# Two small attentions: VectorE's row maxima moved ahead of the step's side work

## The reference

```python
# layer 0, cross attention ("c0"): 32 heads of 16, rotated q and k, no mask
q = (x @ Wq).reshape(b, n, 32, 16); k, v = jnp.split(ctx @ Wkv, 2, axis=-1)
q, k = apply_axial_rope(q, pos_map), apply_axial_rope(k, ctx_pos_map)
w = softmax(einsum('bqhd,bkhd->bhqk', q, k) * scale)
x = layernorm(x + einsum('bhqk,bkhd->bqhd', w, v).reshape(b, n, 512) @ Wout + bout)
# layer 1, self attention ("a1"): 16 heads of 32, 4 key/value groups, causal
x = layernorm(x + causal_softmax_attention(x @ Wq, x @ Wk, x @ Wv) @ Wo + bo)
```

## Time and profile before

| | |
|---|---|
| median of 3 runs | 3154.51 us (3153.39 to 3158.23) |
| the profiled execution | 3152.63 us, span 3150.9 us, mean granted TensorE clock 0.957 |
| busy, share of the span | PE 88%, PE weight loads 65%, DVE 66%, ACT 55%, POOL 49% |
| c0, first to last reduction | 740.7 to 1168.4 us of the span, 256 heads |
| a1, first to last reduction | 1843.8 to 2113.8 us, 128 heads |

### The profile page before, as it was taken

How to read it: one execution, slowest core, us unless ns; L and a number is a source line. 1 busy time by engine, 2 the same in 40 slices (tenths; PEclk the granted TensorE clock), 3 DMA queues, 4 the chain that set the end, 5 groups by cost and what they waited for, 6 DMA issues and landing times. The chain is left out here.

```text
span 3150.9 us, 65193 instructions
## 1 busy us (share of the span) xinstructions
PE 2784.8 (88%) x25058; PEld 2038.7 (65%) x25058; DVE 2068.8 (66%) x4831; ACT 1731.4 (55%) x3747; POOL 1530.0 (49%) x1603
## 2 busy tenths in 40 slices
PE   5999999967889887999999979898999999985787
PEld 4777777744666665777777756666777767752343
DVE  7777777767777775655555546766555665555886
ACT  5555555535777784333333257774444455444896
POOL 3555555534888884544445425561111222213585
PEclk8999999988999997999999989998999999998999
DMA  5000000001000003100000011002011110012000
GB/s 183 21 1 1 1 2 1 1 8 38 2 2 2 2 23 116 35 8 8 1 1 1 1 51 41 23 2 78 7 35 41 41 41 1 1 61 94 14 21 28
DMA packets 47384, 81.94 MB, mean 26 GB/s; under 512 B 5986, under 2 KB 16228, under 8 KB 46948
## 3 DMA queue, kind: packets, MB, share of 16 engines
q1 hardware_dynamic: 47076, 77.77, 7.5%
HBM read 73.44 MB, written 4.19 MB: 25 GB/s over the span
## 5 line engine op out<-in xcount | busy, mean ns | idle before, releaser
L1165 POOL TENSOR_TENSOR c_pT<-c_prob,c_pT 128x512 f16<-128x512 f32 x256 | 295.4, 1169 | 55.5 <-ACT c_pT L1100 54.6
L2097 POOL TENSOR_TENSOR c_prob<-c_prob,c_inv 128x512 f32<-128x512 f32 x128 | 133.0, 1041 | 271.7 <-DVE c_inv L2292 271.7
L1365 ACT ACTIVATE c_prob<-psT 128x512 f32<-128x512 f32 x256 | 155.8, 608 | 80.9 <-PE psT L1294 56.7
L1165 POOL TENSOR_TENSOR a_pT<-a_prob,a_pT 128x384 f16<-128x384 f32 x128 | 120.9, 950 | 157.3 <-ACT a_pT L1100 156.8
L794 DVE SCALAR_TENSOR_TENSOR a_pT<-psT,a_kvh_t,a_pT 128x256 f16<-128x256 f32 (+1 forms) x256 | 94.8, 412 | 145.0 <-ACT a_pT L699 145.0
L491 POOL TENSOR_TENSOR a_q_rot<-a_q_cos,a_q_sin 128x512 f32<-128x512 f32 x64 | 85.2, 1331 | 197.4 <-DVE a_q_sin L812 197.4
L1454 DVE TENSOR_REDUCE c_peak<-psS 128x2 f32<-128x512 f32 x256 | 168.9, 686 | 10.5 <-PE psS L1273 8.1
L1100 ACT CAST c_pT<-c_prob 128x512 f16<-128x512 f32 x256 | 159.3, 623 | 0.0
L2208 ACT ACTIVATE c_prob<-c_prob,c_negmax 128x256 f32<-128x256 f32 x256 | 128.1, 503 | 38.2 <-DVE c_negmax L2284 37.1
L1273 PE MATMUL psS<-c_kS,c_qS 128*128 128x256 f16 x512 | 100.4, 279 | 45.0 <-DVE c_peak L1454 39.9
L1719 POOL TENSOR_TENSOR f_ch<-f_h,f_c 128x256 f32<-128x256 f32 x88 | 72.2, 820 | 134.1 <-DVE f_h L1958 134.1
(11 more groups left out here) (640 smaller groups left out, 11559.4 us busy)
## 6 DMA issues: line engine op xcount, KB each, us to landing
c_feed<-in_L_ffn_w1T SPq DMA_DIRECT2D x16, 512.0 KB, 3.7
c_feed<-in_L_ffn_w2T SPq DMA_DIRECT2D x16, 512.0 KB, 3.7
x_all<-in_x SPq DMA_DIRECT2D x8, 512.0 KB, 6.9
a_ring<-in_L_attn_WqT SPq DMA_DIRECT2D x8, 512.0 KB, 5.8
a_ring<-in_L_attn_WoutT SPq DMA_DIRECT2D x8, 512.0 KB, 4.2
a_feed<-in_L_xattn_Wq SPq DMA_DIRECT2D x8, 512.0 KB, 3.8
c_feed<-in_L_xattn_Wo SPq DMA_DIRECT2D x8, 512.0 KB, 4.3
c_feed<-in_L_ffn_w3T SPq DMA_DIRECT2D x8, 512.0 KB, 3.6
```

The costliest lines, as they stand in the source:

```text
L1165: pool.tensor_tensor(pT[1][:, c % NPH, :], prob[:, c % NPX, :], pT[0][:, c % NPH, :], ALU.subtract)\
L1365: act.activation(prob[:, c % NPX, :], ST[c % 2][:, 0:EW], ACT.Exp).then_inc(s.e_done, 1)
L2097: pool.tensor_tensor(prob[:, h % NPB, :, :], prob[:, h % NPB, :, :], inv[:, h % NPB, :].rearrange("p (n a) -> p n a", a=1).broadcast_to([P ...
```

## The change

In the DVE loop of `small_attention` the block that reduces a head's scores, with a1's `fill_slots`, is moved from behind the side work to the front of the step. Both attentions get it. No instruction, tile or semaphore is added or taken away.

```diff
                 for t in range(FIRST, LAST):
                     if own_pieces(t):
                         own.low(dve, own_pieces(t))
+                    if (found := peak_head(t)) is not None:
+                        b, h = found
+                        rowmax(b, h)
+                        if causal and h % GH == GH - 1:
+                            fill_slots(b, h // GH)
                     for kind, b, n in pieces_at(t - 1):
                         if kind in ("x", "o", "v", "kv") or (kind == "q" and not from_ctx):
                             low(b, kind, n)
...
                         elif kind == "y":
                             measure(b, n)
-                    if (found := peak_head(t)) is not None:
-                        b, h = found
-                        rowmax(b, h)
-                        if causal and h % GH == GH - 1:
-                            fill_slots(b, h // GH)
                     if (found := pv_head(t - 1)) is not None and found[1] % GH == GH - 1:
                         rows_of(found[0], found[1] // GH)
```

## The result

The changed kernel takes 3161.70 us (median of 20 runs, 3154.44 to 3164.57), the kernel before 3154.03 in the same session (20 runs, 3149.77 to 3158.32). The ratio is 1.0021, interval 1.0015 to 1.0028: 6.6 us slower (4.7 to 8.8). That is just beyond what the prediction counted as no change (6.3 us, up to 3160.8), and inside its range. The profiled executions stand at spans of 3160.4 and 3150.9 us, both at a mean granted clock of 0.957.

The account below looks back on a forecast made before the run. No engine was free by much in c0 (PE 88.6, POOL 86.0 of 100 us); PE alone bound a1. c0 -5.5 and a1 +8.8 made +3.3 us: 3155.9 profiled, 3157.8 as the median; range 3147 to 3170.

Parts of the forecast that it names:

- the signs to look for: a1 longer by 6 to 10 us, c0 up to 6 us shorter, c_peak waits below half of 39.9, POOL's gaps smaller.
- c0, slots 26 to 28: Shorter PE stalls before scores let POOL gain 0.85 us in each of five batches: -4.2 us, bounds 0 and 11.
- the faster rival: Clock dips go, POOL's gaps close wholly, all lead-in stalls go, a1 costs 4: -12.4 us, 3142.1; chance 0.13.
- c0, pieces that lose: In c0's slots 11, 19 and 23 PE's pieces wait longer for DVE's side work, mostly covered by POOL: +1.1 us.
- Lead-in (-1.9) and tail (-0.5): Before c0's first softmax, PE's stalls on reductions shrink: -1.9 us, bounds 0 and 5.4; c0's tail stalls: -0.5.
- a1, slots 6 and 7: k and q stacks wait longer for DVE's subtraction and copy, 0.86 in each of seven batches: +6.0 us, the largest term.
- Slots 0 to 2: In a1, x1 and the kv0 projection wait for DVE work now behind the reductions, without cover: +3.4 us.
- Given back: Of a1's 5.6 us of PE waits on the reduction, 1.5 us is taken back: -1.5.
- Slot 15: In a1, behind y0's add, 0.47 us lost in the two batches where PE waits for it: +0.9 us.
- The slower one: Reductions ahead of bank releases paid fully in a1 0 to 7, c0 11 and 19; dips stay: +14.8, 3169.3; chance 0.22.
- That no effect shows: DVE reaches the reduction before scores are ready, and released banks have cover, so order seldom matters: 3154.5 us; chance 0.15.
- The Trainium skill's rule of the most contended engine: Improve the most occupied of Vector, Scalar and GpSimd first; c0 then hangs on GpSimd and gives nothing.

Follow-up runs that it names:

- the picked order: New order everywhere but in c0's slots 11, 18, 22 and a1's slots 0, 1, 5, 6, 7, 14, against the kernel before: 3139.54 us, ratio 0.9957.
- a1 alone: New order in the self attention only, cross attention as in the kernel before: 3163.77 us, ratio 1.0030.
- the lead-in alone: New order only ahead of c0's first batch, everything after as in the kernel before: 3148.72 us, ratio 0.9989.

## Why the prediction was right or wrong

**The outcome.** +3.3 us was forecast and 6.6 found; the direction by stage (c0 shorter, a1 longer) and both sizes of the sum held: c0 -5.5 against -5.3, a1 +8.8 against +11.0. But c0's came out by luck, by two errors of opposite sign. Of the signs to look for, a1's growth (11.0) passed the 6 to 10 us that were named; the others came.

**c0, slots 26 to 28 (-4.2): far too small.** The step that failed is the walk that let POOL gain 1.3 or 0.4 of its 2.2 us and took the middle of it. The gap closes wholly, in every batch, and the dip of the clock at slot 27 with it. With the losing slots spared, c0 gains 11.7 us (416.0) to 13.9 (413.8), 1.3 of it the lead-in's: the upper bound of the term, 11, about reached or a little passed. This was the mechanism of the faster rival. The count was off as well: in the kernel before POOL has a gap of 2 us at slot 27 in four batches (2.02, 2.27, 2.35 and 2.13), not in five, so with the 0.66 of another the cap should have been 9.4. Where the gain passes it, the dips of slot 10 had become fewer too, and they had no term.

**c0, pieces that lose (+1.1): far too small, 8 us in the traces**, about 5 of it at an even clock (0.7 a batch), the rest with dips. The local sizes were right: 0.7 of PE at slot 11 (0.48 and 0.71 found), 0.35 at slot 19 (0.35 found at POOL). What failed is the sentence that ACT passes on 0.3, and that the five batches with a POOL gap at slot 27 absorb the loss. That gap was the one that the change itself closes. Once it is gone, every batch pays: an even batch takes 55.8 us with the new order everywhere and 55.1 with these slots spared.

**Lead-in (-1.9) and tail (-0.5).** The lead-in is 1.3 in the traces without a dip there, and in line with the runs (0.6 to 6.3). The tail wasn't tried.

**a1, slots 6 and 7 (+6.0): the mechanism right, the size 8.0**, because both stalls come in seven or eight batches and the k stack's share is 0.42 rather than 0.24 (0.72 with the new order in slots 6 and 7, 0.30 without; why it falls below the 0.46 of the kernel before wasn't followed up). **Slots 0 to 2 (+3.4): right**, 3.8 in the trace, 5.7 by the runs. **Given back (-1.5):** the wait on a_peak fell by 3.3 us, but the picked order, which keeps the new order in a1's other slots, is no shorter than before: on balance nothing came back. **Slot 15 (+0.9)** wasn't tried alone; the terms of a1 without it already reach 11.8.

**The rivals.** The slower one had the right place (a1 0 to 7, c0 11 and 19) and about the right price for it (10.3 for a1, 6.4 for c0; 11.0 and 8 found), but it was made to hang on POOL's gaps staying open; losses and gain came together. That no effect shows fell with the two halves measured apart. The Trainium skill's rule of the most contended engine (Perfetto Trace Analysis, Identifying the Most-Contended Engine) fits better than I gave it credit for: a shortened instruction of POOL took 18.5 us off c0 (1.6 a batch at an even clock), and with POOL at full work the new order everywhere is worth nothing in an even batch. It doesn't follow that the order of DVE is worth nothing: moved in one slot it took some 9 us off the runs.

**What to do here.** The new order in the lead-in and slot 25 of c0 alone, 3139.62 us: 13 us under before in its session (8.8 to 17.3 by its ratio), and some 20 under the change by the two ratios.

## What to carry to other kernels

Moving one task ahead of the others in an in-order queue trades one wait for another at every step where it isn't urgent: decide it slot by slot, from the row that says who waits at that slot, and not once for the loop. Where a second engine is nearly full, ask of each gain and loss whether it reaches that engine's idle time; and when the gain closes a gap, no loss may be hidden in that same gap any more. Two terms that rest on the same slack are to be summed together, not one by one. And where the clock falls now and then, add up the time at the lower clock in every trace before a difference is put down to the edit, and compare stretches in which it doesn't fall.

## What was unexpected of the hardware

In c0 the granted clock falls to 0.50 for 3.4 us at a time, though PE's matmuls wait no longer than 1.2 us at a stretch for another engine between 800 and 1100 us of the kernel before. In these 300 us it falls six times (at about 858, 916, 944, 974, 1002 and 1087 us), in slots 25 to 27 and 10 of the batches. After the change it is at 0.50 as long (827, 882 for twice the time, 940, 998 and 1097), now in slots 10 and 11 and once in slot 2, and once (992) with the new order in the lead-in and slot 25. In that run a batch (between POOL's rows of slot 20) takes 55.05 us, and 55.6 where the one dip falls; in the kernel before 57.5 to 57.8 with dips and 55.7 in the one batch without. So of the 2.4 to 2.8 us that a batch with dips gained, the batch without them had some 2 already: most of the gain goes together with the dips.

The dips in slots 25 to 27 go with the order of slot 25. With the old order there, the kernel before, a1 alone and the lead-in alone have four each behind the lead-in; with the new order there, none of nine traces with POOL's full work has any, and the lead-in's run and that with slot 25 differ in this slot alone. What a dip costs isn't fixed: in the kernel before a batch with one dip (slot 27) takes 1.8 us more than the one without, in the run with slot 25 a batch with one (slot 10) 0.5. What in the stall before the scores of slot 27 brings the dip, its length or what stands next to it, stays open, and so does why the dips of slot 10 became fewer with it.
